# A second wait on GpSimd ahead of each gathered group, in a two-layer graph network with mixtures of experts

## The reference

```python
x = x + L0_gnn(layernorm(x), edge_weight1, W, b, src, dst)      # agg = segment_sum(feat[src] * eweight) / degree
x = x + L0_ffn(layernorm(x)[None], Wg, bg, bias, W1, b1, W2, b2)[0]   # 8 experts, hidden 512, relu, top 2
x = x + L1_gnn(layernorm(x), edge_weight, Wp, bp, W1, b1, W2, b2, src, dst)  # sqrt(segment_sum(w * relu(x Wp)**2))
x = x + L1_ffn(layernorm(x)[None], router_w, w1, b1, w2, b2)[0]       # 8 experts, hidden 256, gelu, top 2
```

## Time and profile before

| | |
|---|---|
| median of 3 runs | 3251.39 us (3250.32 to 3257.69) |
| profiled execution, its own time | 3246.49 us |
| its span, first to last instruction | 3244.1 us |
| mean granted TensorE clock | 0.894 |
| PE, DVE, ACT, POOL busy | 76%, 55%, 35%, 52% |
| first gather of layer 0, first gather of layer 1 | at 84.93 us, at 1852.97 us |

### The profile page before, as it was taken

How to read it: one execution, slowest core, us unless ns; L and a number is a source line. 1 busy time by engine, 2 the same in 40 slices (tenths; PEclk the granted TensorE clock), 3 DMA queues, 4 the chain that set the end, 5 groups by cost and what they waited for, 6 DMA issues and landing times.

```text
span 3244.1 us, 47395 instructions
## 1 busy us (share of the span) xinstructions
PE 2453.5 (76%) x17987; PEld 1405.7 (43%) x17987; DVE 1779.2 (55%) x4298; ACT 1133.1 (35%) x1835; POOL 1681.3 (52%) x1678
## 2 busy tenths in 40 slices
PE   0136889989989989899999623478787777877897
PEld 0123444544444445444457522344443444444455
DVE  8454666656566566565666433244454544545565
ACT  3022333343343433333545401133232333333455
POOL 3666545454464554544330166566666666666520
PEclk9998999999999999999999855588787888888899
DMA  5532223232232322322220212112212222122110
GB/s 205 202 89 85 80 86 90 81 92 75 85 90 80 92 83 81 89 82 78 68 58 18 81 47 54 41 54 61 59 51 55 62 60 62 51 55 60 50 36 9
DMA packets 115789, 238.02 MB, mean 73 GB/s; under 512 B 30290, under 2 KB 69452, under 8 KB 115044
## 3 DMA queue, kind: packets, MB, share of 16 engines
q0 software_dynamic: 66560, 163.68, 18.2%
q1 hardware_dynamic: 48996, 71.26, 6.4%
HBM read 209.16 MB, written 25.67 MB: 72 GB/s over the span
## 4 chain that ended last, share of the span: by engine, by line
PE 45%; DVE 19%; another core or an unknown queue 16%; issue 12%; ACT 6%; DMA 1%; POOL 1%; DVEq 0%; ACTq 0%; SPq 0%; POOLq 0%
PE psY L714 16%; PE psH L684 14%; DVE hid L1271 4%; PE psM L778 4%; PE psE L674 4%; DVE hsc L1276 3%; PE psE L666 3%; ACT hid L1459 2%; PE psC L691 1%; DVE acc L1110 1%; ACT hsc L1466 1%; DVE wbuf L1022 1%; PE psM L730 1%; DVE mag L968 1%
## 5 line engine op out<-in xcount | busy, mean ns | idle before, releaser
L591 POOL DMA_INDIRECT ring<-table,src_s x1664 | 1653.2, 993 | 1364.3 <-issue 624.9
L714 PE MATMUL psY<-hsc,wbuf 128*128 128x512 f16 (+2 forms) x4032 | 945.3, 371 | 231.7 <-DVE hsc L1276 91.7
L684 PE MATMUL psH<-xnT,wbuf 128*128 128x512 f16 (+2 forms) x4032 | 932.2, 369 | 40.4 <-ACT hid L1459 26.1
L1459 ACT ACTIVATE hid<-psH,b,scl 128x512 f32<-128x512 f32 (+2 forms) x672 | 485.8, 723 | 1289.8 <-PE psH L684 778.5
L1271 DVE TENSOR_TENSOR hid<-hid,psC 128x512 f32<-128x512 f32 (+2 forms) x672 | 415.9, 619 | 573.2 <-ACT hid L1459 408.7
L714 PEld LDWEIGHTS psY<-hsc,wbuf 128*128 128x128 f16 x4032 | 365.2, 101 | 725.6 <-DVE hsc L1276 187.5
L684 PEld LDWEIGHTS psH<-xnT,wbuf 128*128 128x128 f16 x4032 | 383.8, 104 | 373.1 <-issue 79.5
L1110 DVE TENSOR_TENSOR acc<-acc,psE 128x120 f32 (+1 forms) x416 | 98.5, 237 | 656.2 <-remote 477.5
L1276 DVE TENSOR_TENSOR hsc<-hid,hsc 128x512 f16<-128x512 f32 (+2 forms) x672 | 416.3, 619 | 0.4 <-ACT hsc L1466 0.4
L1466 ACT ACTIVATE hsc<-hid 128x512 f16<-128x512 f32 (+2 forms) x672 | 380.1, 566 | 2.9 <-DVE hid L1271 1.9
L674 PEld LDWEIGHTS psE<-ohbuf,ring 128*128 128x128 f32 x1664 | 263.6, 232 | 55.3 <-DMA ring<-table,src_s 22.5
(11 more groups left out here) (155 smaller groups left out, 1764.8 us busy)
## 6 DMA issues: line engine op xcount, KB each, us to landing
ring<-table,src_s POOLq DMA_INDIRECT x1664
wbuf<-w_in SPq DMA_DIRECT2D x2, 4096.0 KB, 16.0
wbuf<-x_in SPq DMA_DIRECT2D x7, 896.0 KB, 11.5
table<-ring SPq DMA_DIRECT2D x7, 896.0 KB, 3.6
feat<-table SPq DMA_DIRECT2D x11, 512.0 KB
xin<-x_in SPq DMA_DIRECT2D x11, 512.0 KB
x_d<-x SPq DMA_DIRECT2D x11, 512.0 KB
xin<-x_d SPq DMA_DIRECT2D x11, 512.0 KB
```

What stands on the lines that cost most here:

```text
L591: pool.indirect_dma_start(out=l.ring[:, g % l.R, k, :], out_offset=None, in_=l.table, in_offset=bass.IndirectOffsetOnAxis(ap=src_s[:, c:c ...
L684: last = mm(psH[n % 2][:, 0:l.TT[t]], l.w1(e, i, k, c), x[:, j, k, 0:l.TT[t]], start=(k == 0 and m == 0), stop=(k == KD - 1 and m == 2))
L714: last = mm(psY[d][:, 0:l.TT[t]], l.w2(e, i, c, d), hsc[n % 2][:, j, 0:l.TT[t]], start=False, stop=(n == l.M - 1 and m == 2))
L1459: f(hid[n % 4][:, 0:l.TT[t]], psH[n % 2][:, 0:l.TT[t]], (ACT.Relu, ACT.Gelu)[l.i], scale=l.un_up, bias=l.b1[:, n // l.HC, n % l.HC:n % l.H ...
```

## The change

POOL waits once more ahead of each group: besides the slot of the ring (unchanged), for the landing of the four DMAs of the group two before. The first two groups of a layer have no such wait. A second no-operation stands behind it. Nothing else is changed.

```diff
+AHEAD = 2
@@
             def gather_group(l, g):
                 if g >= l.R:
                     pool.wait_ge(l.group_summed, g - l.R + 1)
                     hold(pool)
+                if g >= AHEAD:
+                    b = g - AHEAD
+                    pool.wait_ge(l.gathered[b % l.R], 16 * SUB * (b // l.R + 1))
+                    hold(pool)
                 for k in range(SUB):
                     c = g * SUB + k
                     pool.indirect_dma_start(
```

## The result

The changed kernel takes 3272.07 us (median of 11 runs, 3257.09 to 3290.85) against 3251.03 us of the kernel before (11 runs, 3238.53 to 3260.65). The ratio is 1.006, 95% interval 1.004 to 1.0081, so it is slower by some 20 us. The profiled execution took 3271.17 us, with a span of 3268.8 us at a mean granted clock of 0.896, against 3244.1 us and 0.894 before. The forecast was 3254, with a range of 8 in 10 from 3165 to 3275 and 0.37 as the chance of a change within 0.2%. The measured time lies in that range, 3 us under its upper edge, and the change of 0.6% is one of those called "slower by over 0.2%", to which 0.31 was given.

The account below looks back on a forecast made before the run. The prediction took PE's signals, late while POOL prepares DMAs, as what stands out. Profiled 3246.5 us plus 3 for the start and 0 for instructions and steady wait gave 3249.5, about 3254 as median; range of 8 in 10, 3165 to 3275.

Parts of the forecast that it names:

- The two instructions cost 0: On POOL ahead of each group's DMAs: the added wait and no-operation cost nothing visible, taken as 0.
- The bound for POOL run dry: Where POOL has no work prepared: one more 0.30 us gap per group, 124 us of POOL's time, 1.2 us of chain.
- The steady wait costs 0: In steady running: the group two before landed 3.4 us ago, so POOL doesn't run dry; cost 0.
- The start: Layer 0's first groups: slow landing delays groups 2 to 5 and perhaps DVE's third addition; +3 us, from -5.7 to +7.8.
- The bound 126.2: Layer 0's third-group addition on DVE: starts at 126.2 us, 7.8 us later, if PE's signal waits for POOL's run to end.
- The sum: Whole kernel: profiled 3246.5 + 3 + 0 + 0 = 3249.5 us, about 3254 us on the median's scale.
- The start is paid in full: Rival at layer 0's third group: PE's signal held to the run's end, all later work 7.8 us late; 3259 us, chance 0.25.
- A shorter queue frees PE's signals: Rival, layer 1's start: fewer DMAs let in, no signal held over 11.2 us; 3207 us, down to 3165, chance 0.28.
- the long pieces under an unknown releaser: Five chain pieces between 1887 and 2100 us, 14.77 to 35.28 us; sign of the shorter queue if below about 11 us.
- The 239 us: Stretch from layer 1's first gather to its first expert step; a fall of 28 us or more would show the shorter queue.
- More signals are held: Rival at DVE's additions: a tenth of 253 now-unaffected ones held 2.9 us each, 73 us less what is hidden; 3290, chance 0.08.
- the prediction's own mark of 15 us: Forecast wrong if layer 1's starting stretch or DVE's waits for an unknown releaser change by more than some 15 us.

Follow-up runs that it names:

- Layer 1 alone: The changed kernel with the new wait in layer 1 only: 3253.20 us against 3249.48 us of the kernel before, ratio 1.0019.
- e6: The kernel before without the no-operation behind POOL's wait for PE's sum: 3161.91 us against 3253.32 us, ratio 0.9723.
- The start alone: The kernel before with the new wait ahead of groups 2 and 3 of layer 0 only: 3262.38 us against 3249.48 us, ratio 1.0040.
- e4: The changed kernel with the new wait replaced, from group R on, by one always met: 3263.17 us against 3249.48 us of the kernel before, ratio 1.0042.
- the first eleven runs: All follow-up kernels but the last, on three chips, each beside the kernel before; ratios from 0.9695 to 1.0087.
- the twelfth: The kernel before with an always-met wait and no-operation ahead of POOL's wait for PE's sum, on a fourth chip: 2841.52 us against 2844.05 us.
- e8: The kernel before with expert weights loaded after the second group's landing, and the new wait at groups 2 and 3 of layer 0: 3249.99 us against 3253.32 us.

## Where the prediction held and where it failed, point by point

- **The two instructions cost 0: the step that failed.** I read the gap of 0.30 us in runs, where the wait is long met, and took it for the whole price. The bound for POOL run dry was scaled by POOL's 1% of the chain to 1.2 us, and that was the mistake. Where POOL waits for PE, the pair lies between the signal and the DMA that PE will need next. It lengthened the way by 0.061 us at each of some 158 groups of layer 0 and 66 of layer 1, and cost 13.7 us in all (1.0042, 1.0021 to 1.0062). The chain's share of POOL's work says nothing on it, because such a delay shows as somebody's wait.
- **The steady wait costs 0: right.** Layer 1 alone is 1.0019 with an interval that holds 1, and the changed kernel without no-operations is level with e6. And behind the start of layer 0 POOL never waited for a landing in the changed kernel's trace.
- **The start, +3 us between -5.7 and +7.8: mis-sized.** The times of groups 2 and 4 came out within 0.3 us. The bound 126.2 is the right one of the two, and 128.01 was measured: the addition follows the end of POOL's run by 3.2 us, where I took 1.6. I also missed that PE's sum of the third group waits for the addition of the second, whose signal is late as well; the sum still ended 7 us before POOL's run did, so nothing shows that this cost time. The start alone cost 12.9 us (1.0019 to 1.0061, which is 6 to 20 us). That leaves out the +3 of the sum and holds the bound of 7.8. That PE's signal might be prompt, as for layer 1's first group, was not so here.
- **The sum.** 3254 lacks about 14 us for the pair and 10 us for the start; the result lies 18 us above it. That 3272 still falls within the range of 8 in 10 is luck: the edge of 3275 was set with other rivals in mind, and no rival had the pair.
- **The rivals.** "The start is paid in full" had the place, the mechanism and the side of one of the two costs, and 3259 had too little without the other. "A shorter queue frees PE's signals" fell: the long pieces under an unknown releaser are still 14.00 to 31.68 us, all above the 11.2 us that it allowed. From layer 1's first gather to PE's first expert product it is 2093.19 - 1874.00 = 219.2 us, against 2068.82 - 1852.97 = 215.9 us. (The 239 us that the prediction gave this stretch ended at 2092, between the products at 2072.05 and the next at 2100.17; by the first product it is 3.3 us longer in the changed kernel, not 28 us shorter.) Fewer DMAs let in did not shorten what holds a signal. "More signals are held" had a grain of truth, 505.6 against 477.5 us, but e4 has 505.1 too, without any wait for a landing. By the prediction's own mark of 15 us this counts against the forecast.

## What to carry to other kernels

- A wait and a no-operation ahead of an engine's next transfer aren't free because their wait is met: read the time from the releasing signal to the released instruction where the engine stands idle, and multiply by the groups at which it does. Leave the no-operation out where nothing needs it; here that was worth 91 us, more than anything the change was about. To put what is surely met ahead of the wait that ends last brought the way back to 0.739 us; that it saves time wasn't shown.
- A wait on a landing is safe only where landings are quick: look for large loads issued just ahead, by another engine too. Here SP issued them and POOL the gathers.
- Compare only runs of one chip: one trace's dominant wait may be missing on the next.

## What the runs showed of the hardware

- **Late signals were there on three chips and not on a fourth.** On the chips of the first eleven runs the kernel before took 3248 to 3253 us at a granted clock of 0.889 to 0.901, and DVE waited 459.8 to 507.4 us for an unknown releaser at its additions in each profile. On the chip of the twelfth the kernel before took 2844 us at 0.939 to 0.945, and in that run's profile no addition waited so. What differs between the chips, and whether they stay so, is open.
- **A no-operation behind a wait on POOL, and with it a wait that is an instruction of its own, cost 0.48 us** between PE's signal and the first indirect DMA; a further pair of always-met wait and no-operation cost 0.061 us.
- **Landing behind 8 MB of weights**: the first group reached PE 1.8 us after its preparation without them (e8), and at 104.94 us, 15 us after its preparation, with them. The Trainium skill (DMA: Bandwidth & Descriptors, Anatomy of one DMA — SWDGE (gpsimd) path) gives about 2.0 us plus the bytes at 436 GB/s for a DMA, by estimate 2.3 us for the 128 KB of one gather. The trace comes near it where the weights are not ahead, 89.42 - 86.64 = 2.8 us from the start of the group's last DMA to PE, and not behind the load.
